# A two-layer graph network: hops of 101 gathered groups, indices straight from the sorted list, W1's low halves made earlier

## What is computed

```python
h = relu(layernorm(x))
support = h @ weight                      # 256 x 256
h1 = segment_sum(w[e] * support[dst[e]], src[e])       # spmm, hop 1
h2 = segment_sum(w[e] * h1[dst[e]], src[e])            # spmm, hop 2
x = x + relu(hop_w[0] * h1 + hop_w[1] * h2 + h)
h = relu(layernorm(x))
agg = segment_sum(h[src[e]], dst[e])                   # GIN
z = (1 + eps) * h + agg
z = elu(batchnorm(z @ W1 + b1)); z = elu(batchnorm(z @ W2 + b2))
z = elu(batchnorm(z @ W3 + b3)); out = x + z @ W4 + b4 # 512, 1024, 512, 256 wide
```

## Time and profile before

| | us |
|---|---|
| median of 3 runs | 4348.43 |
| the runs | 4345.99 to 4348.55 |
| the profiled execution | 4354.81 |
| its span, first to last instruction | 4353.3 |
| mean granted TensorE clock | 0.928 |

### The profile page before, as it was taken

The page is one execution under the profiler, slowest core; times in us unless marked ns, Lnnn a source line. Parts: engine busy times, 40 slices in busy tenths (PEclk is TensorE's granted clock), DMA queues, the critical chain, the costliest instruction groups (busy, mean ns, idle before and its releaser), DMA issues. The chain is left out here.

```text
span 4353.3 us, 47248 instructions
## 1 busy us (share of the span) xinstructions
PE 3221.4 (74%) x15687; PEld 2674.9 (61%) x15687; DVE 1863.5 (43%) x4616; ACT 794.5 (18%) x1957; POOL 2578.5 (59%) x2612
## 2 busy tenths in 40 slices
PE   6699677777777677777777745666666666998998
PEld 5288566555556555555555545555555555887887
DVE  6899343333333333333333322222222224556766
ACT  4099000000000000000000000000000002555657
POOL 0077677777777677777777757777777774001000
PEclk9899899999999899999999977788888777999999
DMA  4000333443434433333333345333333332223323
GB/s 145 1 5 6 90 104 109 123 122 114 122 118 119 102 104 108 113 109 108 107 113 108 107 87 162 106 105 104 104 104 105 105 104 80 101 91 128 100 63 118
DMA packets 207710, 438.01 MB, mean 101 GB/s; under 512 B 45953, under 2 KB 126293, under 8 KB 207421
## 3 DMA queue, kind: packets, MB, share of 16 engines
q0 software_dynamic: 121856, 324.04, 26.4%
q1 hardware_dynamic: 85677, 111.75, 7.9%
HBM read 376.09 MB, written 59.53 MB: 100 GB/s over the span
## 5 line engine op out<-in xcount | busy, mean ns | idle before, releaser
L1993 PE MATMUL ps<-work 128*128 128x256 f32 x6528 | 1536.4, 390 | 513.6 <-DMA work<-table_hop,idx 509.9
L829 POOL DMA_INDIRECT work<-table_hop,idx x1632 | 1583.2, 970 | 529.8 <-issue 489.6
L1993 PEld LDWEIGHTS ps<-work 128*128 128x128 f32 x6528 | 1227.7, 193 | 810.5 <-DMA work<-table_hop,idx 361.2
L874 POOL DMA_INDIRECT work<-table_gin,idx x832 | 793.1, 953 | 286.1 <-issue 229.5
L2077 PE MATMUL ps<-work 128*128 128x128 f32 x3328 | 570.1, 342 | 414.3 <-DMA work<-table_gin,idx 384.9
L2077 PEld LDWEIGHTS ps<-work 128*128 128x128 f32 x3328 | 525.3, 248 | 484.4 <-DMA work<-table_gin,idx 335.3
L1472 DVE TENSOR_SCALAR work<-iota,w_hi,edge_buf 128x256 f32<-128x256 bf16 x1632 | 548.2, 409 | 1.7 <-issue 1.1
L1644 DVE TENSOR_TENSOR sum_b<-sum_b,ps 128x256 f32 x104 | 43.9, 422 | 800.8 <-PE ps L2077 800.8
L985 ACT COPY idx<-w 128x8 int32<-128x8 int32 x204 | 40.0, 197 | 1844.9 <-PE ps L1993 1844.2
L1484 DVE TENSOR_TENSOR big<-big,ps 128x512 f32 x102 | 70.2, 688 | 680.5 <-PE ps L1993 680.5
L1484 DVE TENSOR_TENSOR sum_b<-sum_b,ps 128x512 f32 x102 | 70.2, 688 | 651.7 <-PE ps L1993 651.7
(11 more groups left out here) (246 smaller groups left out, 2681.4 us busy)
## 6 DMA issues: line engine op xcount, KB each, us to landing
work<-table_hop,idx POOLq DMA_INDIRECT x1632, 2.8
z_dram<-sum_b SPq DMA_DIRECT2D x24, 964.0 KB, 4.1
sum_b<-z_dram SPq DMA_DIRECT2D x24, 964.0 KB, 5.2
work<-table_gin,idx POOLq DMA_INDIRECT x832, 2.8
big<-x SPq DMA_DIRECT2D x12, 512.0 KB, 6.0
table_hop<-work SPq DMA_DIRECT2D x12, 512.0 KB, 2.9
table_hop<-sum_b SPq DMA_DIRECT2D x12, 512.0 KB, 3.5
x_dram<-big SPq DMA_DIRECT2D x12, 512.0 KB, 3.4
```

Of the source, the lines that this page charges most:

```text
L829: pool.indirect_dma_start(hop_rows[:, par, t, :], None, table[n], bass.IndirectOffsetOnAxis(idx[:, k % HR, t:t + 1], 0)).then_inc(rows_in[ ...
L874: pool.indirect_dma_start(rows[:, par, t, :], None, table[2], bass.IndirectOffsetOnAxis(idx[:, q, t:t + 1], 0)).then_inc(rows_in[par][half ...
L1993: mm = pe.matmul(ps[:, HWIN * par + b, 0:D], hot[:, par, t, b * P:(b + 1) * P], hop_rows[:, par, t, :], start=(t == 0), stop=(t == GT - 1))
```

## The change

HGROUPS goes from 102 to 101 and PACE from 8.5 to 8.4, so each hop has one group less and the plan's places are a little closer. With an odd number of groups the buffer of a group is now taken from its number over both hops (g % 2), and the counts of landed rows are kept the same way. The hop gathers take their index columns from `idx_sorted` directly; ScalarE's copies, their three buffers and their semaphore go, and POOL waits once for the list. On POOL the two low halves of W1 come ahead of the wait for the GIN table; TensorE waits for each of them ahead of the first chunk's product that needs it, and no longer ahead of GIN group 0.

```diff
-HGROUPS = 102
+HGROUPS = 101
...
-PACE = 8.5
+PACE = 8.4
 HWIN = 2
-HR = 3
...
             def gather(n, k):
                 g = n * HGROUPS + k
-                par = k % 2
-                pool.wait_ge(hop_idx, g + 1)
+                par = g % 2
...
-                                                bass.IndirectOffsetOnAxis(idx[:, k % HR, t:t + 1], 0)
+                                                bass.IndirectOffsetOnAxis(idx_sorted[:, k * GT + t:k * GT + t + 1], 0)
...
-                pool.wait_ge(sort_turned, 2)
+                pool.wait_ge(sorted_ready, 1)
...
+            for k in range(K1):
+                split_low(w1_sb, w1_split, k, k)
             pool.wait_ge(ln_stored, 32 * FULL)
             pool.wait_ge(c_turned, CHUNKS)
...
-            def low_of_w1(j, u):
-                if isinstance(j, int) and j == 0 and u < K1:
-                    split_low(w1_sb, w1_split, u, u)
-
             with pool.If(near):
-                over_groups_and_z1(pool, gin_gather, low_of_w1)
+                over_groups_and_z1(pool, gin_gather, lambda j, u: None)
             with pool.Else():
-                for k in range(K1):
-                    split_low(w1_sb, w1_split, k, k)
...
-            def fill_hop(n, k):
-                g = n * HGROUPS + k
-                if not (n == 0 and k < HR):
-                    act.wait_ge(hop_mm, 2 * (g - HR + 1))
-                act.wait_ge(sorted_ready, 1)
-                act.copy(idx[:, k % HR, :], idx_sorted[:, bass.ds(k * GT, GT)]).then_inc(hop_idx, 1)
-
...
             def hop2_step(k):
-                fill_hop(1, k)
...
-                over_hop(act, lambda k: fill_hop(0, k))
...
-                    last = dve.tensor_scalar(hot[:, k % 2, t, :], iota[:, :], loc_sorted[:, at_], w_sorted[:, at_],
+                    last = dve.tensor_scalar(hot[:, g % 2, t, :], iota[:, :], loc_sorted[:, at_], w_sorted[:, at_],
...
             def hop_group(n, k):
                 g = n * HGROUPS + k
-                par = k % 2
+                par = g % 2
...
-                    pe.wait_ge(rows_in[par][half], 16 * HT * (n * HGROUPS // 2 + k // 2 + 1))
+                    pe.wait_ge(rows_in[par][half], 16 * HT * (g // 2 + 1))
...
                 if m == 0:
+                    if first:
+                        pe.wait_ge(w_split, k + 1)
                     pe.wait_ge(sums_split, K1 * c + k + 1)
...
-            pe.wait_ge(w_split, K1)
```

More of the change, by code:

```diff
@@ L109 @@
 assert BT * P + NK * (SLOT - 1) <= REG * P * SLOT and BGROUPS <= P and BT % 2 == 0
-assert SLOT == GT and HGROUPS % 6 == 0 and 8 + int(PACE * (FULL - 1)) < HGROUPS - 1 + 1 and LGOES + int((PACE - 2) * (FULL - 2)) + 1 >= int(PACE * (FULL - 1)) and LSTEP * LGOES == LTILES
+assert SLOT == GT and 8 + int(PACE * (FULL - 1)) < HGROUPS and LGOES + int((PACE - 2) * (FULL - 2)) + 1 >= int(PACE * (FULL - 1)) and LSTEP * LGOES == LTILES
 def over_chunks(eng, step):
@@ L477, in gnn @@
         loop_added = sem("loop_added")
-        hop_idx = sem("hop_idx")
         rows_in = [[sem(f"rows_in{par}{half}") for half in range(2)] for par in range(2)]
```

## The result

The changed kernel takes 4308.14 us (median of 4 runs, 4305.52 to 4311.79) against 4348.49 for the kernel before: ratio 0.9909, 95% interval 0.9897 to 0.9921, or 40.4 us less. The forecast was 4315.6 us, 32.8 us less. The profiled execution took 4311.79 us (span 4310.3), 43.0 us less than the profiled one of before.

What follows compares the result with a forecast made beforehand. POOL's row of indirect gathers was taken to bound the kernel. Gains of 11.82 + 13.80 + 0.3 + 6.9 = 32.8 us took the profiled 4354.81 to 4322.0, less 6.4 for the median: 4315.6 us, range 4308 to 4324.

Steps and rivals of the forecast that it cites:

- What bounds the kernel: From 456 to about 3640 us: the number of POOL's gathers times 1.26 us, plus places where their row is broken.
- The fast path stays: On-chip fit test: 12841 blocks of non-loop edges fit 101 groups, 87 places left, so the slow loop does not run.
- Part 1, one group fewer: Ends of both hops: dropping the all-padding group gains 11.82 us in hop 1 and 13.80 in hop 2.
- upper end: Ends of both hops: 30.7 us, with 1.9 us each from usual landing and 1.3 us from TensorE's half group.
- about 8 us: Start of the GIN stage: TensorE's first GIN matmul expected about 8 us after the first gather.
- The explanation of the late landing: Ends of the hops: padding gathers, which fetch one and the same row, land late, up to 8.0 us against 2.8.
- Part 2, indices from the list: Start of hop 1: without ScalarE's copies the first gather comes 0.3 us sooner; steady state and wide tile cost nothing.
- (b): Hop gathers: the wide index tile costs 14 ns each, +22.6 us, 4338.2 us; chance 0.05.
- (c): Hop gathers: index reads near VectorE's one-hot columns lengthen each from 0.953 to 1.02 us, +81 us, 4397 us; chance 0.05.
- Part 3, the splits: Start of the GIN gathers: W1 splits hidden ahead of the table wait gain 6.9 us, between 4.6 and 7.0.
- rival (a): GIN start: a slipped split or other hold-up still breaks the gathers, gain 0 to 4.6, 4318 to 4322.5 us; chance 0.09.
- rival (e): Ends of the hops close up further than group 100's rows show, time below 4309 us; chance 0.06.

Runs made afterwards that it cites:

- hops101_alone: Kernel before with 101 groups, PACE 8.4 and the parity over both hops, ScalarE's copies and the place of W1's splits kept: 4318.76 us, ratio 0.9927.
- pace_8p4_102: Kernel before with only PACE changed from 8.5 to 8.4, still 102 groups: 4344.74 us, ratio 0.9999.
- the four companions: Kernel before, 102 groups, one edit each: direct index columns 4350.07 us, POOL's splits early 4343.1, TensorE's wait late 4345.89, PACE 8.4 4344.74.
- the second chip: The changed kernel run again, unaltered, against the kernel before (4347.81 us there): 4306.72 us, ratio 0.9907.

## Why the prediction was right, and where it was short

**What bounds the kernel:** right. Every gain of the change is either a gather that is not issued, a gather that is shorter, or a break in the row of gathers that closes.

**The fast path stays:** right; the count of 12841 blocks held.

**Part 1, one group fewer:** the mechanism was right and the size short: 25.6 us forecast, 32.5 in the two profiled executions, 32.4 in the medians of `hops101_alone`. The step that failed is the reading of group 100 in the kernel before as the future last group. Its time from last gather to last add was 12.5 and 11.6 us there; as the last group, in the changed kernel and `hops101_alone`, it takes 8.8 to 10.4 and 9.0 to 9.2. The text had this as its upper end and split it in two. One half, rows landing in the usual time when nothing is queued behind them, was wrong in size: TensorE started 4.92 and 5.37 us after the last gather and not 5.62 and 6.00, a gain of 0.7 and 0.6 us instead of 1.9, because the group's own 87 free slots hold its rows up; only spreading them brings 2.7 us. The text's 3.8 for the usual case added the gather's own 0.96 us to a landing of 2.8 us that is counted from the gather's start and holds it already, so its upper end would have been 2.8 and 3.2 us. The same slip is in the sign "about 8 us" for the first GIN matmul, which came 6.71 us after the first gather. The other half, TensorE's time for the half group, brought the larger part (6.9 to 5.5 us in hop 1, 5.6 to 3.9 in hop 2), and it is not the change's for certain, since it depends on where the slow clock falls. The third piece, 2.5 us in hop 2's row of gathers, was not foreseen: the sum took 10.05 us for a group, and did not see that up to eleven gathers of 1.9 us, beside x1, and those beside one-hots set a spread of a few us, by how they fall; ten and not eleven were hit in the changed kernel. `pace_8p4_102` leaves open how much of it belongs to 101 groups. The view cited for a gather's length, up to 1965 ns, had shown that such gathers exist.

**The explanation of the late landing** by the one padding row was only argued then. It is shown now: spreading the padding leaves 6.5 and 6.7 us at the ends of the hops with 102 groups, where the four companions have 11.8 to 12.1 and 12.9 to 14.5.

**Part 2, indices from the list:** right. 0.26 us forecast as 0.3, nothing in the steady state, no price of the wide tile. Rivals (b) and (c) are refuted by the gathers' 969 ns against 970. But the first gather's 1.24 us was not a cost of starting that stays: it became 1.48 us, since it ends 0.86 us after VectorE's tensor_tensor in both kernels. The term holds by the second gather, which came 4.41 us after the list and not 4.66; why it moved with the first start is not shown.

**Part 3, the splits:** right to 0.02 us. The splits ran from 2546.52 to 2549.11, and POOL still waited 1.94 us for the table: the room of 1.5 us was there. They overlap VectorE's one-hots by 0.4 us and took 1.3 us each; the lower end, with the split behind all one-hots, did not come about, and rival (a) with it.

**The sum** missed by 7.5 us of the medians, with 4308.14 at the very edge of the range: some 6 to 7 from the hops, the rest within what two sets of runs differ by (the same pair gave 41.1 us on the second chip). It was rival (e), the ends of the hops closing up further, that came out by its size; it had been given 0.06, and deserved more, since the text had itself found 1.9 and 1.3 us in each hop for it.

## What to carry to other kernels

Where one engine's row of equal instructions sets the time, count them, and then read the places where the row breaks: at the end of a loop the last item pays for landing, for the consumer and for the consumer's clock, so removing it is worth more than its share. Padding that points all slots at one row is not free even with weight 0, so point it at different rows; and cut a long two-input VectorE instruction beside a row of gathers into short ones, since a gather stands for nearly the whole of it.

## What the runs showed that was not expected

- Gathers whose 128 rows are all the same row landed 5.8 to 8.0 us after their start where 2.7 is usual, each later than the one ahead of it; with 128 different rows the last half of a hop starts 2.7 us after the last gather instead of 8.9.
- An indirect gather on POOL stands while VectorE runs a scalar_tensor_tensor with two inputs in SBUF: 1.75 to 1.97 us beside one of 1.23 us, 1.3 to 1.4 beside 0.7, 1.0 to 1.15 beside 0.42, if it starts after that instruction. It ends 0.8 us after the instruction that ran at its start. The Trainium skill, page "SBUF — State Buffer", section "Who interferes with whom", has such an instruction contend with POOL's reads of SBUF, which agrees; the same section infers that plain descriptor generation is not stalled by tensor_tensor, and no run here tests a DMA without indices beside one, but the gathers, which read their indices from SBUF, are stalled by both two-input forms: the first gather of hop 1 took 1.48 us and ended 0.86 us after a tensor_tensor.
- TensorE gave a last half group of 3.72 or 5.38 us in executions of one kernel, by the level of its granted clock, where it had stood 2.3 to 2.5 us for rows ahead of one of the last two halves; with spread padding the last halves took 3.7 us in both hops of all three kernels.
